# A 6-layer windowed-attention stack, run twice: another order of every engine's work, its loops written out, and bare increments on TensorE

## What is computed

```python
x = x + retention(layernorm(x))        # L0_attn_a
x = x + stack(layernorm(x))            # L0_ffn, first run
x = x + mixer(layernorm(x))            # L0_attn_b, a scan over 512 steps
x = x + stack(layernorm(x))            # L0_ffn, second run, same weights
```

```python
def attn_layer(x):                     # 16 heads of 64, windows of 32
    q, k, v = split(x @ Wqkv)          # 128 -> 3 * 1024
    q, k = rotary(l2norm(q) * qs), rotary(l2norm(k) * ks)
    # each window of 32 queries sees its own and the previous 32 keys
    sim = q @ k2.T * 8; p = softmax(where(mask, -max, sim))
    return (p @ v2) @ Wo
def ffn_layer(x):
    h = layernorm(x) * g + bln
    a, gate = split(h @ W1 + b1)       # 2 * 341
    return a * gelu(gate) @ W2 + b2
for i in range(6):
    x = attn_layer(shift_tokens(x)) + x
    x = ffn_layer(shift_tokens(x)) + x
```

## Time and profile before

| what | us |
|---|---|
| median of 3 runs (3636.82 to 3646.73) | 3645.67 |
| the profiled execution | 3648.2 |
| its span, first to last instruction | 3646.4 |
| PE busy, DVE busy | 3373.7, 3341.6 |
| ACT busy, POOL busy | 2049.2, 2706.3 |

### The profile page before, as it was taken

One profiled execution on the slowest core, in us unless ns is written; L12 is line 12 of the kernel. 1 busy time (PEld: TensorE's weight loads), 2 busy tenths in 40 slices (PEclk: granted clock), 3 DMA queues, 4 the chain that ended last, 5 costly groups with the idle time before them and its releaser, 6 DMA issues. The chain is left out here.

```text
span 3646.4 us, 153624 instructions
## 1 busy us (share of the span) xinstructions
PE 3373.7 (93%) x60144; PEld 2186.3 (60%) x60144; DVE 3341.6 (92%) x11899; ACT 2049.2 (56%) x3659; POOL 2706.3 (74%) x2440
## 2 busy tenths in 40 slices
PE   6799999999999999987699689999999999999997
PEld 4366666666666666652466446666666666666664
DVE  6899999999999999965799799999999999999995
ACT  2456666656665666644422155666666566666663
POOL 1788888888888888843144288888888888888882
PEclk9899999999999999998799699999999999999999
DMA  1233333333333333320000123333333333333332
GB/s 44 61 89 83 74 89 75 90 78 79 91 76 76 87 80 71 72 66 16 1 1 0 36 49 88 79 89 79 74 93 75 77 84 82 73 89 77 72 72 65
DMA packets 151851, 250.83 MB, mean 69 GB/s; under 512 B 42688, under 2 KB 73408, under 8 KB 150976
## 3 DMA queue, kind: packets, MB, share of 16 engines
q1 hardware_dynamic: 151104, 240.75, 27.7%
HBM read 38.21 MB, written 1.05 MB: 11 GB/s over the span
## 5 line engine op out<-in xcount | busy, mean ns | idle before, releaser
L608 PE MATMUL stack_work<-stack_w_qkv,stack_xst 128*128 128x512 f32 x2304 | 1173.6, 615 | 26.9 <-ACT stack_sq L881 16.7
L1337 POOL TENSOR_TENSOR stack_roped<-stack_rot_c,stack_rot_s 128x512 f32<-128x512 f32 x768 | 980.6, 1289 | 260.1 <-DVE stack_rot_s L1082 135.0
L1347 POOL TENSOR_TENSOR stack_roped<-stack_roped,stack_rnorm 128x512 f32<-128x512 f32 x768 | 791.5, 1044 | 162.4 <-DVE stack_rnorm L1114 162.4
L881 ACT ACTIVATE stack_sq<-stack_work 128x512 f32<-128x512 f32 x768 | 457.3, 595 | 735.0 <-DVE stack_rot_s L1082 727.5
L1080 DVE TENSOR_TENSOR stack_rot_c<-stack_work,rot_tables 128x512 f32<-128x512 f32 x768 | 517.0, 673 | 56.5 <-PE stack_work L608 52.0
L608 PEld LDWEIGHTS stack_work<-stack_w_qkv,stack_xst 128*128 128x128 f32 x2304 | 387.3, 193 | 300.5 <-issue 226.5
L1082 DVE TENSOR_TENSOR stack_rot_s<-stack_work,rot_tables 128x512 f32<-128x512 f32 x768 | 519.3, 676 | 1.1 <-issue 1.1
L1091 DVE TENSOR_REDUCE stack_ssq<-stack_sq 128x8 f32<-128x512 f32 x768 | 512.4, 672 | 3.3
L1125 DVE CUSTOM_DVE_ANT_0 stack_s_m<-stack_bank_s,band 128x64 f32<-128x64 f32 x3072 | 469.5, 215 | 30.1 <-PE stack_bank_s L632 26.4
L617 PEld LDWEIGHTS stack_work<-ident,stack_roped 128*128 128x128 f32 x3072 | 354.1, 141 | 167.4 <-issue 143.5
L617 PE MATMUL stack_work<-ident,stack_roped 128*128 128x128 f32 x3072 | 436.4, 277 | 19.3 <-ACT stack_sq L881 11.6
(11 more groups left out here) (255 smaller groups left out, 5093.2 us busy)
## 6 DMA issues: line engine op xcount, KB each, us to landing
stack_v_even<-stack_v_nat SPq DMA_DIRECT2D x768, 128.0 KB, 2.4
stack_p_pairs<-stack_p_turned SPq DMA_DIRECT2D x1536, 64.0 KB
stack_w_qkv<-table_ffn_qkv SPq DMA_DIRECT2D x192, 96.0 KB
stack_w_o<-table_ffn_wo SPq DMA_DIRECT2D x12, 512.0 KB, 3.9
stack_w<-table_ffn_w SPq DMA_DIRECT2D x12, 384.0 KB, 3.2
stack_w<-table_ffn_w SPq DMA_DIRECT2D x12, 192.0 KB, 3.0
x_outer<-L_attn_a_X SPq DMA_DIRECT2D x4, 256.0 KB, 8.1
ret_xpos<-table_xpos SPq DMA_DIRECT2D x1, 1024.0 KB, 7.5
```

Of the source, the lines that this page charges most:

```text
L608: pe.matmul(work[(BANK["p_" + c][T] + g.row) % 4][:, :], xst[:, g.row, P * T:P * (T + 1)], w_qkv[:, g.half, col:col + 512], start=True, st ...
L881: act.activation(sq[:, i % 2, :], work[(BANK["p_" + c][T] + g.row) % 4][:, :], ACT.Square).then_inc(done["squared_" + c], 1)
L1337: pool.tensor_tensor(roped[:, i, T % 2, :], rot_c[:, i % 2, :], rot_s[:, i % 2, :], ALU.add).then_inc(done["roped_" + c], 1)
L1347: pool.tensor_tensor(r, r, rnorm[:, T % 2, i, :].unsqueeze(2).broadcast_to([P, 8, HD]), ALU.mult).then_inc(done["united_" + c], 1)
```

## The change

1. The order of the calls in `slot` is another one on PE, ACT, DVE and POOL, and the SP queue spreads values and probabilities one slot later in most slots. The table `BANK` is another one, since banks follow from the order. The work itself is the same.
2. `slots` writes all 112 slots out, and so does the SP queue with its layers. The loops, their register instructions and the increments of `apart` are gone.
3. A table `SETTLE` and a function `settle` put bare increments of `passed` in front of visits on PE: 3,520 in all, before 97 visits of 384. From tile 9 of a run on, nearly to its end, they stand before `weigh` of every odd tile, alternately 37 and 33.

```diff
+SETTLE = {
...
+    "weigh": (
+        (0, 0, 0, 1, 0, 52, 0, 45, 0, 37, 0, 33, 0, 37, 0, 33, 0, 37, 0, 33, 0, 37, 0, 33,
...
-        FIRST_IN, LAST_IN = "k0", "v0"
+        FIRST_IN, LAST_IN = "q0", "v0"
...
-            run_slots(0, 0, 0, 0, 16)
-            with eng.Fori(0, 2) as pair:
-                run_slots(32 * pair + 16, 8 * pair + 4, 2 * pair + 1, 1, 32)
-            run_slots(16 * (DEPTH - 1), 4 * (DEPTH - 1), DEPTH - 1, 1, 16 + 16)
+            run_slots(0, 0, 0, 0, TILES + 16)
...
             def layer_loads(layer, first, last):
                 for n in range(16):
-                    spread_values(layer, n)
-                    spread_probs(layer, n)
+                    if n % 4 == 0:
+                        spread_values(layer, n - 1)
+                        spread_probs(layer, n - 1)
+                        spread_probs(layer, n)
+                    elif n % 4 == 1:
+                        spread_values(layer, n - 1)
...
-            with sp.Fori(1, DEPTH - 1) as layer:
+            for layer in range(1, DEPTH - 1):
...
+            def settle(t, T, g, kind):
+                if live(t):
+                    for _ in range(SETTLE[kind][run][t]):
+                        pe.sem_inc(passed, 1)
...
+                    settle(*at(9), "weigh")
                     wait(pe, "ot_set", N - 10)
                     weigh(*at(9), 0)
                     weigh(*at(9), 1)
...
-                    wait(dve, "united_k1", t - 2)
+                    wait(dve, "united_q1", t - 2)
```

More of the change, by code:

```diff
@@ L342 @@
 GELU_TABLE = "gelu_and_others"
+SETTLE = {
+    "scores": (
[8 rows of a table added]
+    ),
+    "weigh": (
[8 rows of a table added]
+    ),
+}
 Group = namedtuple("Group", ("number", "layer", "row", "pair", "half"))
@@ new lines, in slot @@
+                    wait(pe, "kept_q0", N - 6)
+                    up(of(4), "lin", 1)
+                    wait(pe, "kept_k1", N - 6)
+                    project(*at(4), "k1")
+                    wait(pe, "v_out1", N - 7)
+                    up(of(4), "lin", 0)
+                    settle(*at(6), "scores")
+                    wait(pe, "masked0", N - 7)
+                    wait(pe, "masked1", N - 7)
+                    scores(*at(6), 0)
+                    scores(*at(6), 1)
+                    wait(pe, "mid_set", N - 10)
@@ new lines, in slot @@
+                    sum_squares(*at(4), "q1")
+                    rotate(*at(3), "q0")
+                    sum_squares(*at(4), "k1")
+                    sum_probs(*at(7), 0)
+                    norms(*at(4), 0)
+                elif T == 1:
+                    rotate(*at(4), "k0")
+                    invert(*at(8), 0)
+                    sum_probs(*at(8), 1)
+                    mid(*at(11))
+                    invert(*at(8), 1)
+                    norms(*at(5), 1)
+                    sum_squares(*at(4), "q0")
+                    mask_max(*at(7), 1)
+                    mask_max(*at(7), 0)
+                    turn_probs(*at(8), 1)
+                    norms(*at(5), 2)
+                    turn_probs(*at(8), 0)
+                    mid(*at(10))
+                    norms(*at(5), 3)
+                    hidden(of(4), 1)
+                    sum_squares(*at(4), "k0")
+                    rotate(*at(4), "k1")
+                    sum_probs(*at(7), 1)
+                    hidden(of(4), 0)
+                    sum_probs(*at(7), 0)
+                    rotate(*at(4), "q1")
+                    sum_squares(*at(4), "k1")
+                elif T == 2:
+                    rotate(*at(4), "k0")
+                    invert(*at(8), 1)
+                    invert(*at(8), 0)
+                    hidden(of(4), 2)
+                    if is_slot(N, TILES + 14):
+                        for s in range(BATCH - 1):
+                            add_to_outer(s)
+                    sum_squares(*at(5), "q1")
+                    mask_max(*at(7), 0)
+                    mask_max(*at(7), 1)
+                    sum_squares(*at(4), "k0")
+                    norms(*at(5), 0)
```

500 lines of the change are left out of this document (234 added, 266 removed), and 15 rows, old and new, of the table SETTLE.

## The result

The changed kernel takes **4198.25 us** (median of 4 runs, 4196.84 to 4208.24) against 3641.24 for the kernel before, measured beside it (4 runs, 3634.68 to 3646.73). The ratio is 1.154 [1.1519, 1.156], 557 us. I had forecast 3624, with 3740 as the upper end.

The account below looks back on a forecast made before the run. PE and DVE were taken as nearly full, PE needing 15.51 us a tile after the change. From 3648.2 us, 13 and 9 came off: 3626, or 3624 against the median; forecast band 3595 to 3635, full range 3560 to 3740.

Parts of the forecast that it names:

- What one takes no row shows ... so I take 55 ns, near the lower end.: Price of one bare increment on PE's sequencer, bounded by 51 ns and 0.1 us; 70 in four tiles make 3.85 us.
- PE idle ahead of `weigh` of odd tiles for over 1 us: Sign in the profile after that would show the forecast wrong because increments are dear.
- The sequencer's lead of 1.5 us: PE's sequencer runs ahead of the array, hiding 1.5 us of increments at each of two places in four tiles.
- the increments bind: Rival, chance 0.24: at 0.1 us each, increments put 4.0 us in four tiles on PE's path, giving 3775 us.
- So that no such wait is left: While PE stands at increments others free their banks, so PE's 0.3 us wait a tile vanishes; gain 13 us.
- The borders: Borders of 256-row blocks stop drifting; one regular stall of 1.6 us in four tiles, where `scores` directly follows `weigh`.
- the same as before, 0.39 against 0.40: PE's stalls at block borders, in us a tile before and after the change: same cost, only regular.
- The order. I cost it at nothing: New order of calls: later spreads and steps moved back a slot were taken to be covered, at no cost.
- a new wait: Rival, chance 0.08: the regular stall before `scores` reaches DVE's masks whole, 0.40 us a tile, about 3700 us.
- The loops, 9 us: Writing the loops out removes two turns of the loop at 4.5 us each.
- which cost nothing: The `apart` increments and register rows lie beside matmuls, so removing them was taken to gain nothing.
- the borders don't matter: Rival, chance 0.04: block crossings are mostly hidden, stalls stay and increments add 40 us less 9, giving 3677 us.

Follow-up runs that it names:

- a_half: The changed kernel with half of each count of bare increments (18 and 16 in place of 37 and 33): 3815.28 us, ratio 1.0482 to the kernel before.
- a_dup: The changed kernel with 9 and 8 repeats of the first `weigh` matmul in place of 36 and 32 increments: 3750.75 us, ratio 1.0307.
- a_none: The changed kernel without any bare increments, new order and written-out loops kept: 3701.18 us, ratio 1.0164 to the kernel before.
- a_pair: a_none with two projections moved between `weigh` and `scores`, so that no two visits follow each other directly: 3615.76 us, ratio 0.9943.
- b_out: The kernel before with its loops written out and without the `apart` increments, old order, no bare increments: 3607.86 us, ratio 0.9896.
- b_pd2: b_out with some `weigh` matmuls issued twice and a few increments, holding block borders at good rows: 3593.14 us, ratio 0.9869.
- b_bad2: b_pd2 with more duplicates before run 0's first `weigh`, so that borders stand 90 rows later, at bad rows: 3674.07 us, ratio 1.0098.
- a_pairdup: The changed kernel with the moved projections of a_pair and the repeated first `weigh` matmul of a_dup: 3653.87 us, ratio 1.0031.
- a_pd2: a_pairdup with the first 9 and 8 different `weigh` matmuls issued twice in place of one repeated: 3652.91 us, ratio 1.0037.

## Why the prediction was wrong, step by step

- **"What one takes no row shows ... so I take 55 ns, near the lower end."** This is the step that failed. The runs and the trace of after show 150 ns, outside both of my bounds. The row's own 51 ns is no distance to the next row. The chain at 805.1 to 805.3 printed distances rounded to 0.1, and I argued it down ("those wait as well") when it was already too low. With 150 ns in place of 55 my own formula gives 10.5 - 3.0 = 7.5 us in four tiles, 360 us, and the a_half dose nearly the same, 370. "PE idle ahead of `weigh` of odd tiles for over 1 us", my own sign of a dear increment, is what the trace shows.
- **The sequencer's lead of 1.5 us**: near, 1.4 by a_half and 1.2 by the pauses.
- **What a pause does to the clock**: not in the sum at all. It is 130 to 150 us here. I took the clock of 1.00 as given, and never asked what PE's standing still for several us would do to it.
- **The rival "the increments bind"** had the mechanism that decided, with a chance of 0.24 and a price of 3775 at 100 ns. Its mechanism was right and its size was off, by the two points above; with 150 ns it would have said 3945.
- **"So that no such wait is left"**, 13 us gained: not so. PE's pause is no time in which the others catch up; DVE waits 192 us of 1200 for projections that stand behind the pause.
- **The borders**: the regular stall came where I put it and in the size I gave (1.76 us, once in four tiles, in a_dup). In the changed kernel itself it is smaller (12 stalls, 6.8 us in 1200); there 44 of the 46 visits ahead of it are slow, so that the block lasts longer. The stall is 0.3 us on average behind the 30 slowest of these and 1.5 and 1.7 behind the two that are not slow. But "the same as before, 0.39 against 0.40" compared only totals. a_none has 0.44 us of stalls a tile against 0.32 in before, and a_pair against a_none shows that the pair costs 80 us.
- **"The order. I cost it at nothing"**: wrong by 0.027 between a_none and b_out, about 97 us, of which the pair is 80. The rival "a new wait", with a chance of 0.08, had the regular stall reach DVE whole; it does, though through the projections behind `scores` and not through the masks. The place was in my own list of rows; I had given it to the borders' account and not compared it with the written-out kernel.
- **The loops, 9 us**: the change's second part is worth 36, but only about 5 by the turns (0 to 10, so the 9 itself isn't excluded). The rest is `apart`, "which cost nothing".
- **The rival "the borders don't matter"**, by the Trainium skill ("Runtime: NRT & Kernel Launch", Instruction fetch mechanics: crossing a block is "mostly hidden"): it would give b_pd2 and b_bad2 the same time, and they differ by 81 us. Its other consequence, that the increments are pure loss, is what happened; though not by that rule.

Added up in ratios (they must close, since each is the step from one kernel to the next): the loops written out -0.010, the new order +0.027, the increments +0.138 gives 1.154. A sharper test is my own sum with the prices put right: 3624 - 40 + 360 for the increments, + 150 for the clock, + 97 for the order, - 27 for the loops is 4164; the remaining 34 us no run assigns. (The chances of the three slower rivals add up to 0.36, not 0.37.)

Open: why a_pairdup and a_pd2 both cost about 33 us more than a_pair. Their sums of filler and stalls in 1200 us are 28 and 17 us above a_pair's, which would be some 70 and 45 us in the whole, and in both DVE's wait for `down` rose from 11.2 to 24.9 and 24.2 us in 1200; no run tells why. Open also is how `apart` costs its 24 us on PE, and what keeps a bare increment from following another in less than 150 ns.

## What to carry to other kernels

A filler is priced by how far its rows *start* apart, not by how long a row is, and it is worth one look at a few of them alone before 3,520 are placed. If the borders of instruction blocks hurt, first break up stretches in which two runs of small matmuls follow each other (here 2.2%, for two projections moved), and fill, where needed, with work that the array does side by side, or with increments behind long matmuls. A pause of 4 us on TensorE is paid twice here, the second time in the clock of what follows, and so were the longest stalls of about 2 us.

## What the runs showed of the hardware

- From one bare semaphore increment on PE's sequencer to the next it is 150 ns, though its row is 51 ns long.
- Behind a pause of 4.06 us the granted clock was 0.50 for a whole visit of 3.57 us (`after`), and it was 0.50 soon after a stall of 2.22 us (a_none). With two matmuls of 128 columns in the pause it was 1.00 in it and 0.73 behind.
- One small matmul repeated, on one tile of the array, passed every 56 ns; those of a visit, on four tiles in turn, every 15.
- PE stalled at borders of 256-row blocks where the block's own work was short. Where two visits followed each other the stalls were 0.6 to 2.8 us in 40 of 46 places of a_none; in b_pd2, where each block holds 4.2 us of work by my count, 2.0 us were left in 1200.
